# One layer of attention and mixture of experts on one core: order of the prologue, form and place of the slots' weights, place of the last stores, lead of the routed rows

## The reference

```python
xn = _layernorm(x)
q = rope(xn @ Wq + bq); k = rope(xn @ Wk + bk); v = xn @ Wv + bv      # 16 heads of 16
attn = softmax(where(causal, -inf, q @ k.T / 4))
a = (attn @ v) @ Wo + bo
scores = softmax(xn @ gate_w.T)
topk_w, topk_ids = top_k(scores, 6); topk_w /= sum(topk_w)
comb[token, topk_ids] = topk_w
routed = sum over e of comb[:, e] * ((silu(g_e) * u_e) @ w_down_e.T)   # g_e, u_e = xn @ w_gate_up_e.T
shared = (silu(sg) * su) @ ws_down.T
out = x + a + routed + shared
```

## Time and profile before

| | |
|---|---|
| three runs | 740.82, 740.29, 731.63 us, median 740.29 |
| profiled execution | 730.91 us, its span 729.0 us |
| granted clock of PE, mean over the span | 0.974 of full |
| PE, DVE, ACT, POOL busy | 676.1, 435.6, 319.3, 360.6 us |

### The profile page before, as it was taken

One profiled execution on the slowest core, in us unless ns is written; L12 is line 12 of the kernel. 1 busy time (PEld: TensorE's weight loads), 2 busy tenths in 40 slices (PEclk: granted clock), 3 DMA queues, 4 the chain that ended last, 5 costly groups with the idle time before them and its releaser, 6 DMA issues.

```text
span 729.0 us, 18953 instructions
## 1 busy us (share of the span) xinstructions
PE 676.1 (93%) x4876; PEld 405.8 (56%) x4877; DVE 435.6 (60%) x1184; ACT 319.3 (44%) x830; POOL 360.6 (49%) x376
## 2 busy tenths in 40 slices
PE   7999999989999999999999999998888798899857
PEld 4745777755555555555555555554445465455534
DVE  4588999975454454454455555543557656667534
ACT  2653222224444444444444444443556445556332
POOL 3000000258587677586687878466155434554450
PEclk9999999999999999999999999999999979999879
DMA  8420001236877968869776785469865545554221
GB/s 253 136 62 0 1 1 34 85 120 198 265 218 223 308 200 270 289 199 298 233 222 210 213 255 174 100 140 326 277 195 175 166 136 170 167 173 122 75 73 44
DMA packets 77120, 124.02 MB, mean 170 GB/s; under 512 B 11047, under 2 KB 51176, under 8 KB 77080
## 3 DMA queue, kind: packets, MB, share of 16 engines
q1 hardware_dynamic: 41206, 59.89, 27.4%
q0 software_dynamic: 15872, 46.16, 21.7%
q10 hardware_dynamic: 20002, 17.47, 7.2%
HBM read 85.73 MB, written 37.75 MB: 169 GB/s over the span
## 4 chain that ended last, share of the span: by engine, by line
PE 82%; another core or an unknown queue 4%; DVE 4%; issue 3%; DMA 2%; ACT 2%; SPq 1%; DVEq 1%; ACTq 0%
PE pair L1152 22%; PE pair L1194 13%; PE pair L1138 5%; PE pair L1125 5%; PE bank L1161 4%; PE pair L1028 4%; PE pair L1176 4%; PE bank L1257 3%; PE pair L1221 3%; PE pair L1239 2%; PE bank L1289 2%; PE pair L1231 2%; PE pair L1033 2%; PE pair L1213 2%
## 5 line engine op out<-in xcount | busy, mean ns | idle before, releaser
L433 POOL DMA_INDIRECT lower<-xn_rows,idx_all x128 | 135.9, 1061 | 215.6 <-DVE idx_all L823 121.7
L1152 PE MATMUL pair<-space,work 128*64 (+1 forms) x768 | 167.0, 467 | 11.1 <-issue 4.8
L1194 PE MATMUL pair<-lower,work 88*64 x512 | 121.8, 379 | 1.3 <-ACT work L615 0.7
L833 DVE TENSOR_TENSOR work<-work,pair 128x176 f32<-128x176 f32 x160 | 53.8, 337 | 105.7 <-ACT work L600 79.7
L1152 PEld LDWEIGHTS pair<-space,work 128*64 128x64 f32 x768 | 67.5, 137 | 83.8 <-issue 52.5
L600 ACT ACTIVATE work<-pair 128x176 f32<-128x176 f32 x160 | 50.9, 318 | 125.2 <-PE pair L1152 66.0
L1194 PEld LDWEIGHTS pair<-lower,work 88*64 88x64 f32 x512 | 69.5, 136 | 48.2 <-issue 8.3
L635 ACT ACTIVATE pT<-pair 128x768 f32<-128x768 f32 x64 | 51.9, 811 | 88.5 <-PE pair L1243 63.1
L1152 PE MATMUL pair<-wqkv_sb,work 128*64 128x352 f32 x256 | 89.4, 472 | 0.0
L914 DVE TENSOR_REDUCE negm<-pair 128x2 f32<-128x256 f32 (+1 forms) x128 | 64.9, 551 | 30.9 <-PE pair L1221 26.6
L607 ACT ACTIVATE lower<-pair 128x256 f32<-128x256 f32 x128 | 49.2, 384 | 75.4 <-PE pair L1194 75.2
(11 more groups left out here) (186 smaller groups left out, 1217.7 us busy)
## 6 DMA issues: line engine op xcount, KB each, us to landing
space<-wgu SPq DMA_DIRECT2D x66, 352.0 KB
y_rows<-lower ACTq DMA_DIRECT2D x128, 128.0 KB
qk_all<-qk_rows SPq DMA_DIRECT2D x64, 256.0 KB
lower<-wdn SPq DMA_DIRECT2D x66, 176.0 KB
qk_rows<-space POOLq DMA_DIRECT2D x32, 256.0 KB
qk_rows<-qk_all POOLq DMA_DIRECT2D x32, 256.0 KB
x_all<-x SPq DMA_DIRECT2D x4, 512.0 KB, 7.4
xn_rows<-qk_all SPq DMA_DIRECT2D x16, 128.0 KB, 1.8
```

The source lines that it names most:

```text
L433: po.indirect_dma_start(xg[:, r % XB, :], None, xn_rows[:, :], bass.IndirectOffsetOnAxis(idx_all[:, r:r + 1], 0)).then_inc(xg_in[r % XB], 16)
L833: dve.tensor_tensor(hid[:, u % 2], sg[:, u % 2], pair[u % 2][:, F:2 * F], ALU.mult).then_inc(hid_ok, 1)
L1152: last = pe.matmul(pair[u % 2][strip, 0:2 * F], xgT[u][:, c, strip], n, start=c == 0, stop=c == EC - 1, skip_group_check=True)
L1194: last = pe.matmul(pair[u % 2][strip, 512:512 + E], hT[:, u % 2, c, strip], n, start=c == 0, stop=c == 1, skip_group_check=True)
```

## The change

- SP loads x in five pieces (2, 2, 4, 4 and 4 tiles), and the first two groups of the normalisation are two tiles each. The nine constants of `c_in_act` are moved from ACT's queue to SP's, behind the projection weights and ahead of wo. ACT takes one root of a constant before its first real one.
- `slot_weights` still has three steps for a token tile, but a step is now two instructions of 128x64, each of which compares, multiplies and sums for one chosen expert, with the sum as a second output. `WEIGH_AT` puts four steps beside each of the tiles 21 to 28, and none beside 29 and 30, where before three or four stood beside each of the tiles 21 to 30.
- In `beside` the copy of the expert's weights comes ahead of `list_beside`. PE loads the registers of the first four routed tiles beside shared tile 24 (`EXPERTS_AT`) and no longer after the last shared tile.
- `LATE` is gone: all 64 stores of `qk_rows` lie between the gathers.
- `ROWS_FROM` goes from -2 to -6 and `LATER` from 4 to 1.

```diff
-WEIGH_AT = sorted([-2] * 2 + 2 * list(range(1, 20, 3)) + 3 * list(range(21, 31)) + [22, 24])
+WEIGH_AT = sorted([-2] * 2 + 2 * list(range(1, 20, 3)) + 4 * list(range(21, 29)))
-LATER = 4
-ROWS_FROM = -2
+LATER = 1
+ROWS_FROM = -6
-LN_GROUPS = ((0, 4), (4, 8), (8, 16))
+LN_GROUPS = ((0, 2), (2, 4), (4, 8), (8, 16))
+X_LOADS = (0, 2, 4, 8, 12, 16)
...
             sp.dma_start(wqkv_sb[:, :, 0:QK], w[:, :, 0:QK]).then_inc(w_in, 16)
+            sp.dma_start(bqk_sb[:], bqk.to_broadcast([P, QK])).then_inc(c_in_act, 16)
...
+            sp.dma_start(iota_f[:], iota).then_inc(c_in_act, 16)
             sp.dma_start(wo_sb[:], wo.rearrange("(c p) n -> p c n", p=P)).then_inc(c_in, 16)
...
-            steps = [(n, k) for n in range(PIECES) for k in range(PIECE_STEPS if n < LATE else ROPE_STEPS)]
+            steps = [(n, k) for n in range(PIECES) for k in range(PIECE_STEPS)]
...
-            for n in range(LATE, PIECES):
-                late(n)
...
+            act.wait_ge(ones_ok, 1)
+            act.activation(col[0:NE, 0:1], ones_c[:], ACT.Sqrt)
             root(0)
...
-                if step == 0:
-                    i = dve.tensor_tensor(part, key[:, t].unsqueeze(1).to_broadcast([P, TOPK, NE]),
-                                          top[:, t, 0:TOPK].unsqueeze(2).to_broadcast([P, TOPK, NE]), ALU.is_equal)
-                elif step == 1:
-                    i = dve.tensor_tensor(part, part, comb[:, t].unsqueeze(1).to_broadcast([P, TOPK, NE]), ALU.mult)
-                else:
-                    i = dve.tensor_reduce(w6[:, t, 0:TOPK], part, AX.X, ALU.add)
+                for k in range(2 * step, 2 * step + 2):
+                    i = dve.scalar_tensor_tensor(part[:, k], key[:, t], top[:, t, k:k + 1], comb[:, t], ALU.is_equal,
+                                                 ALU.mult, accum_out=w6[:, t, k:k + 1])
                 i.then_inc(dpair, 1)
...
             def beside(i):
-                list_beside(i)
                 if i + 3 in early[:2]:
                     up_copy(i + 3, (i + 3) % XB)
+                list_beside(i)
...
+                if i == EXPERTS_AT:
+                    for u in range(XB):
+                        load_expert(SHARED_TILES + u, u)
```

48 lines of the change are left out of this document (21 added, 27 removed).

## The result

The changed kernel took 744.96 us in the median of 20 runs (734.8 to 750.9), the kernel before 736.02 us (726.95 to 744.83, 20 runs). The ratio is 1.0113 with a 95% interval of 1.0083 to 1.0144: slower by 1.1%, where 0.9% faster was forecast. A ratio in this document takes only executions of each kernel that are within 1.5% of its fastest, so it can differ from the ratio of the medians. The profiled execution has a span of 743.4 us against 729.0.

The account below looks back on a forecast made before the run. PE was taken to bound the kernel, so only its idle or slow stretches count; +0.5 +1.0 -3.5 -2.4 -2 = -6.4 us from the median of 740.3 gave 733.9 us (724.5 on the profiled level), range 718 to 745.

Parts of the forecast that it names:

- What bounds the kernel: Whole kernel: PE bounds it, so a change is worth only what it takes from PE's idle time or slow stretches.
- Stores between the gathers: Routed stage: four bursts at 0.3 us cost +1.2, the end gains -3.6; -2.4 us in all, between 0 and -4.
- a rule by which the full 3.6 us come back: Routed stage: DMA engines serve queues packet by packet, so stores beside weight loads take their share; 3.6 us return in four portions.
- weights or gathers late: Rival, routed stage: POOL falls behind or stores push out expert weights, 10 us in all, time 742 to 744; chance 0.09.
- The passage: Shared to routed tiles: both weight copies come earlier and the next pair starts sooner; -3.5 us, range -1 to -4.5.
- The remark about the earlier release of POOL: Passage: POOL, released earlier, could hit another DVE copy through the shared ports, giving back about 1 us.
- Slots' weights: Beside shared tiles 21 to 28: new DVE instructions at 0.24 us each; with register loads +1.0 us, between 0 and +2.5.
- The rival of dear instructions: Slots' weights: the small instruction takes 0.38 us, not 0.24, costing 10.5 us over eight tiles; time 744, chance 0.13.
- Prologue: Kernel start: PE's queue hides the earlier tiles, constants issued later on SP cost 0 to 2 us; taken as +0.5.
- Start of the attention: Attention start: ninth q and k load no longer late, PE's half-clock stretch after it gone; -2 us, between 0 and -5.
- Routed rows: Attention: gathers lead sums by seven slots, not six, with nothing to win; zero, between -1 and +2 us.
- The unexplained gaps: Rival, attention: ACT's seven unnamed waits, 22.8 us, vanish (711 us, chance 0.08) or grow by half (745, 0.03).

Follow-up runs that it names:

- red_stores: Kernel before with all q and k stores between the gathers and DVE's expert-weight copies made by a reduction (maximum): ratio 1.0064, routed stage 350.2 us.
- stores_only: Kernel before with one part of the change, all stores of q and k between the gathers: ratio 1.0118, routed stage 355.1 us.

## Why the prediction was wrong

**What bounds the kernel** was right: the losses are where PE idles or slows down. One mark of failure that I had named came about: PE's idle time in the routed stage grew by 10.0 us. The forecast of 733.9 us and its direction were wrong, and the median of 744.96 us lies at the very end of the range, 745.

**Stores between the gathers: the step that failed.** I took a burst at 0.3 us, since PE's whole idle time in the stage left at most 2.1 for each. The term was +1.2 us for four bursts. The first 56 pairs, where they stand, took 18.8 us more in the profiled execution and 17.3 as a part alone. The bound was no bound: it was drawn from bursts of one and two stores, and the change makes them of three. I had counted 136 steps for 104 and used it for POOL's time only, and I had not asked what POOL's work does to DVE's copies in this stage. Even dealt out singly the moved stores cost 3.8 us with the reduction. The prediction states a rule by which the full 3.6 us come back, and I had given it no weight. A warning was in the trace: the first burst's pairs of 6.10 and 6.08 us, where the median pair took 5.43. The rival "weights or gathers late" had the sign and the size (10 us) at 0.09, but not the cause. POOL waited for PE still 61.8 us in all (64.9), and every gather of the changed kernel whose landing can be read from the trace had landed 1.7 us or more before its rows were transposed. That the late load and the late pairs would go was right: the last pairs take 5.4 us and less, a gain of 4.4 us for 3.6 forecast.

**The passage** was right in the order of the work and too large in size. The -2.7 in the table, for a forecast of -3.5, is luck in part: 1.3 us of the forecast were a lower clock that I read from one profile, and seven kernels with the same passage ran it at full clock. Against them the passage gains 1.1 us with its cost of 0.4 beside tiles 21 to 28 counted (forecast with the register loads at +1.0). The remark about the earlier release of POOL decided the rest. Alone, the passage gained nothing, with a copy of 2.19 us; in the changed kernel POOL's two steps of 157.4 and 158.8 us were over when the next large copy began at 160.5. With copies that POOL can't hold up it gained 0.8. So what I priced at 1 us was worth up to the whole gain. The Trainium skill, SBUF — State Buffer, section "Who interferes with whom", says that a reduction never contends with GpSimd on this chip while a copy can. The trace of red_stores agrees: its reductions of 128x704 took 0.87 to 0.89 us, 0.876 in the mean of the row above, and none was longer.

**Slots' weights**: 0.21 us from one to the next, for 0.24 forecast. The rival of dear instructions is out.

**Prologue**: +2.6 for +0.5, and for another reason. The number is from one profile and within what the old prologue once showed (78.3), but four of the five profiles with the new prologue have the hole, and one of fifteen with the old. I wrote that PE's queue hides the earlier tiles, and did not follow ACT's order. The second group's root stands behind the copies of the first, so the group of two opened a hole of 1.65 us in PE, and PE's clock fell after it. The constants were not late.

**Start of the attention**: the late load went, as forecast. stores_only gained 3.7 us there; in the whole change it is covered by a wait of 10.10 us of the unexplained kind, and start and body together are 0.4 shorter. **Routed rows**: zero forecast, zero found. **The unexplained gaps** moved and kept their sum. What they are stays open, and nothing was tried on them.

## What to carry to other kernels

When work is dealt out by a step count, count how many steps of a kind fall in a row before and after, and price the row and not the step: here three stores where one or two stood turned a cheap burst into a dear one. The same stores dealt singly cost only what they had cost at their old place, once no copy could be held up. Split a stage where work was moved from and to before reading its total, since a gain at one end hides a loss at the other. When a small gain is read against one profile of before, look at the other kernels of the study that have the same code in that place: here 1.2 us and a stretch at the lower clock lay between them. Look at the lengths of one instruction in the trace beside each engine's neighbour: DVE copies of 0.53 us that take 2 us beside POOL hide a wait, and a form of instruction that is slower alone can be faster in company. Moving one engine's work earlier in a prologue helps only if every engine in the chain gets it earlier, else the bounding engine gets a hole, behind which its clock fell here.

## What was not expected of the hardware

- Register loads from SBUF (TENSOR_LOAD) on DVE took 0.42 us in the median and up to 2.3 us before and 2.7 after; the six longest of either profile stood within 4 us behind a store. On PE they took up to 1.93 us.
- A copy of 128x704 on DVE took 0.53 us with POOL's arithmetic cut short and up to 2.19 beside it. The same copy as a maximum over an axis of one took 0.88 every time and made the whole kernel 0.5% faster (ratio 0.9949, 0.9913 to 0.9986).
- An instruction with a second, summed output cost 0.21 us at 128x64; the accumulator's read of 0.08 lies beside it.
- A hole in PE of 1.65 us behind a dense stretch was followed by ten microseconds at a granted clock of 0.60 to 0.68. Five profiles have such holes, of 1.3 to 2.0 us, and a clock of 0.50 to 0.68 from 17.2 to 22.5 us.
- In nine of the twenty profiles PE's clock fell once between the first shared tile and the end of the routed stage, for 3.4 us, to its lower level. Each time there was a hole of 0.79 to 1.83 us in PE that ended within 1.5 us of the fall.
